# Moving part of a layer transition from VectorE to GpSimd, with new activation tables, gate slots and last PSUM banks

## The reference

```
xn = layernorm(x)
s = attention(xn)              # softmax over theta(qk), theta from sigmoid, tanh and relu
g = silu(xn + moe(layernorm(xn)))   # 8 experts, top 1, and a shared one
x = x + s * g                  # residual of layer 0
xn = layernorm(x)              # per row: mean, variance
s = mamba(xn)                  # conv, silu, softplus(delta), dA = exp(delta*A), scan over 512 steps,
                               # 16 states, 256 channels; y = sum_n C_n * h_n, + D*xv, @ W_out
g = silu(down(silu(gate(xn)) * up(xn)))   # int weights / 127
x = x + s * g
```

## Time and profile before

| | us |
|---|---|
| median of 3 runs | 743.29 |
| lowest, highest | 740.79, 745.15 |
| the profiled execution | 744.14 |
| its span | 742.3 |
| TensorE busy | 662.6 |
| VectorE busy | 630.6 |
| ScalarE busy | 514.7 |
| GpSimd busy | 476.0 |

### The profile page before, as it was taken

The page is one execution under the profiler, slowest core; times in us unless marked ns, Lnnn a source line. Parts: engine busy times, 40 slices in busy tenths (PEclk is TensorE's granted clock), DMA queues, the critical chain, the costliest instruction groups (busy, mean ns, idle before and its releaser), DMA issues.

```text
span 742.3 us, 12844 instructions
## 1 busy us (share of the span) xinstructions
PE 662.6 (89%) x3973; PEld 497.4 (67%) x3973; DVE 630.6 (85%) x1042; ACT 514.7 (69%) x1080; POOL 476.0 (64%) x292
## 2 busy tenths in 40 slices
PE   1898999999799998769999999999999999986885
PEld 0884556556555553346887887877868878876775
DVE  5768877777666663999999999999999999999996
ACT  1465666666544444789898799898998987987452
POOL 1000564000044554155898999999999999999997
PEclk9999999999999999989999999999999999999998
DMA  7900110001112215544634736365376356363300
GB/s 210 293 1 0 43 40 32 0 0 28 60 47 72 66 58 76 102 176 144 142 86 155 160 85 197 105 161 145 82 210 148 86 172 157 89 206 92 72 1 28
DMA packets 43432, 74.75 MB, mean 101 GB/s; under 512 B 6264, under 2 KB 30208, under 8 KB 41968
## 3 DMA queue, kind: packets, MB, share of 16 engines
q1 hardware_dynamic: 31744, 48.35, 20.3%
q0 software_dynamic: 9904, 25.12, 16.8%
q10 hardware_dynamic: 1728, 0.57, 0.3%
HBM read 46.01 MB, written 9.67 MB: 75 GB/s over the span
## 4 chain that ended last, share of the span: by engine, by line
PE 33%; POOL 29%; DVE 12%; issue 12%; DMA 9%; ACT 4%; SPq 1%; POOLq 0%; ACTq 0%; DVEq 0%
POOL nfT_all L1254 22%; DMA delta_e<-delta_e 7%; PE psum L1304 5%; PE psum L699 4%; PE psum L592 3%; PE psum L622 3%; PE psum L723 3%; POOL accP L1187 2%; POOL du L1239 2%; DVE xnT_all L1812 2%; PE psum L613 2%; PE psum L600 2%; PE psum L602 2%; PE psum L632 1%; PE psum L711 1%
## 5 line engine op out<-in xcount | busy, mean ns | idle before, releaser
L1812 DVE TENSOR_TENSOR_SCAN xnT_all<-psum,nfT_all 128x1024 f32<-128x1024 f32 x128 | 288.2, 2276 | 7.5 <-issue 5.3
L1304 PEld LDWEIGHTS psum<-W_out,xnT_all 128*128 128x128 f32 x2048 | 241.9, 194 | 45.5 <-issue 34.7
L1304 PE MATMUL psum<-W_out,xnT_all 128*128 128x128 f32 x2048 | 247.0, 278 | 14.7 <-DVE acc L1828 10.9
L1504 ACT ACTIVATE psum<-delta_e,A 128x511 f32<-128x511 f32 x256 | 167.0, 693 | 32.0 <-DVE xnT_all L1812 32.0
L1254 POOL TENSOR_TENSOR nfT_all<-nf_rows,du 128x1024 f32<-128x1024 f32 x63 | 148.4, 2478 | 22.2 <-DVE nfT_all L1894 21.6
L1254 POOL TENSOR_TENSOR nfT_all<-attn_all,du 128x1024 f32<-128x1024 f32 x64 | 161.7, 2687 | 0.0
L573 POOL DMA_INDIRECT moe_dram<-xnT_all x39 | 37.7, 967 | 120.0 <-ACT xnT_all L829 120.0
L562 POOL DMA_INDIRECT xs_dram<-nf_rows,pos x32 | 33.1, 1033 | 78.3 <-DVE pos L883 59.2
L1828 DVE SCALAR_TENSOR_TENSOR acc<-psum,in_rows,acc 128x128 f32<-128x128 f32 x224 | 61.8, 337 | 0.9
L1304 PE MATMUL psum<-vo_all,W_taps 128*128 128x512 f32 (+3 forms) x128 | 59.2, 593 | 0.7 <-ACT vo_all L1536 0.7
L1304 PE MATMUL psum<-vo_all,wgu 128*128 128x512 f32 x96 | 47.6, 618 | 6.6 <-DVE hff L1907 5.6
(11 more groups left out here) (227 smaller groups left out, 1163.8 us busy)
## 6 DMA issues: line engine op xcount, KB each, us to landing
nf_rows<-bt_dram SPq DMA_DIRECT2D x32, 512.0 KB, 5.0
attn_all<-bt_dram SPq DMA_DIRECT2D x32, 512.0 KB, 4.1
delta_e<-rl_ab POOLq DMA_DIRECT2D x7, 1024.0 KB, 8.1
res_all<-early POOLq DMA_DIRECT2D x7, 1024.0 KB, 7.2
delta_e<-delta_e POOLq DMA_DIRECT2D x7, 512.0 KB, 7.4
xs_dram<-attn_all SPq DMA_DIRECT2D x4, 645.0 KB, 8.0
xnT_all<-xs_dram SPq DMA_DIRECT2D x39, 64.5 KB, 1.9
x_all<-in_x_dram SPq DMA_DIRECT2D x8, 256.0 KB, 6.7
```

What stands on the lines that cost most here:

```text
L1304: return nc.tensor.matmul(o, l, r, start=start, stop=stop)
L1504: ins = nc.scalar.activation(dA[:, i % RA, k, 1:L], delta[:, p, h, 1:L], ACT.Exp, scale=A[:, h, 2 * q + k:2 * q + k + 1])
L1812: nc.vector.tensor_tensor_scan(hring[:, i % R, :, :].rearrange("p n l -> p (n l)"), dA[:, i % RA, :, :].rearrange("p n l -> p (n l)"), dbx ...
```

## The change

GpSimd takes the gate products of batches 3 to 7 and the adds of batches 5 to 7. `g_w` gets four slots in the place of two. In the first preparation the touch of Exp is replaced by an explicit load of the table set `natural_log_exp_and_others`; `roots(2)` moves ahead of `skip_out` and `C_out` and is followed by a second such load; `turned(2)` moves behind the first `decay`. `gates(6)` moves ahead of `conv_silu(0, 1)`. VectorE's `clear()` moves to the start of its list, and `shifts(2)` moves from ahead of `drives` to behind `conv_gate(1)` of round 0. In the last round states 12 and 13 go to banks 4 and 5, which are free once `gate()` has run, in the place of 6 and 7.

```
-            g_w = over[:, 4 * L:6 * L].rearrange("p (r l) -> p r l", l=L)
+            GW = 4
+            g_w = over[:, 0:GW * L].rearrange("p (r l) -> p r l", l=L)
+            def state_bank(b, n):
+                return bank[bM[n % 2]] if b == NB - 1 and n >= NS - 4 else bank[Gb[n % 2]]
 # GpSimd
+                def gated(i):
+                    pool.wait_ge(F["si"], i + 1)
+                    pool.wait_ge(F["sg"], i)
+                    pool.wait_ge(F["x1"], i - 1)
+                    nc.gpsimd.tensor_tensor(sg[:, i % 2, :], g_w[:, i % GW, :],
+                                            attn_all[:, i * TPB:(i + 1) * TPB, :].rearrange("p j d -> p (j d)"),
+                                            ALU.mult).then_inc(F["sg"], 1)
+                def added(i):
+                    pool.wait_ge(F["sg"], i + 1)
+                    pool.wait_ge(F["x1"], i)
+                    x_rows = x_all[:, i * TPB:(i + 1) * TPB, :].rearrange("p j d -> p (j d)")
+                    nc.gpsimd.tensor_tensor(x_rows, x_rows, sg[:, i % 2, :], ALU.add).then_inc(F["x1"], 1)
                 for b in range(NB):
                     ...
+                    if b == NB - 2:
+                        gated(3)
+                gated(4)
+                for i in range(5, NB):
+                    gated(i)
+                    added(i)
 # TensorE, project(n)
-                        drained(pe, b, n - 2)
+                        if b == NB - 1 and n >= NS - 4:
+                            pe.wait_ge(S["G1"], at(b, "G1", 1))
+                        else:
+                            drained(pe, b, n - 2)
 # ScalarE, gates(i)
-                    if i >= 2:
-                        act.wait_ge(F["sg"], i - 1)
+                    if i >= GW:
+                        act.wait_ge(F["sg"], i - GW + 1)
 # ScalarE, first_preparation
                         ssm_out()
-                        nc.scalar.activation(touch[:, :], eps[:, :], ACT.Exp)
+                        nc.scalar.preload_act_table_set("natural_log_exp_and_others")
                         ...
+                        roots(2)
+                        nc.scalar.preload_act_table_set("natural_log_exp_and_others")
                         skip_out()
                         C_out()
-                        roots(2)
-                        turned(2)
                         act.wait_ge(F["col"], 1)
                         decay(b + 1, 1 - p, 0, True)
+                        turned(2)
                         decay(b + 1, 1 - p, 1)
 # ScalarE, start
                 gates(5)
+                gates(6)
                 conv_silu(0, 1)
-                gates(6)
                 gates(7)
 # VectorE, first_preparation
                         conv_gate(0)
-                        residual(4)
+                        moments_of(3)
+                        added(4)
                         conv_gate(1)
-                        residual(5)
+                        moments_of(4)
                         norms(1)
-                        residual(6)
+                        moments_of(5)
+                        moments_of(6)
                         ...
-                        residual(7)
+                        moments_of(7)
                         moments(2)
                         ...
-                        shifts(2)
 # VectorE, round_, behind conv_gate(1)
+                    if not end:
+                        shifts(2)
 # VectorE, start
+                clear()
                 residual(0)
                 moments(0)
                 norms(0)
-                clear()
                 residual(1)
                 residual(2)
                 moments(1)
-                residual(3)
+                added(3)
```

More of the change, by code:

```diff
@@ L1329, in project @@
                         pe.wait_ge(S["scan"], at(b, "scan", 2 * q + 2))
-                        drained(pe, b, n - 2)
+                        if b == NB - 1 and n >= NS - 4:
+                            pe.wait_ge(S["G1"], at(b, "G1", 1))
+                        else:
+                            drained(pe, b, n - 2)
                         for j in range(TPB):
                             for h in range(KH):
-                                ins = mm(bank[Gb[n % 2]][:, j * P:(j + 1) * P],
+                                ins = mm(state_bank(b, n)[:, j * P:(j + 1) * P],
                                          hring[:, (2 * q + h) % R, n % 2, j * P:(j + 1) * P], W_out[:, h, :],
@@ L1509, in gates @@
                     act.wait_ge(s_moe[i % 2], 16 * (i // 2 + 1))
-                    if i >= 2:
-                        act.wait_ge(F["sg"], i - 1)
-                    nc.scalar.activation(g_w[:, i % 2, :], res_all[:, i * TPB:(i + 1) * TPB, :]
+                    if i >= GW:
+                        act.wait_ge(F["sg"], i - GW + 1)
+                    nc.scalar.activation(g_w[:, i % GW, :], res_all[:, i * TPB:(i + 1) * TPB, :]
                                          .rearrange("p j d -> p (j d)"), ACT.Silu).then_inc(F["si"], 1)
@@ L1557, in scale_state @@
                     for j in range(TPB):
-                        ins = nc.scalar.activation(ts(i)[:, j, :], bank[Gb[n % 2]][:, j * P:(j + 1) * P], ACT.Copy,
+                        ins = nc.scalar.activation(ts(i)[:, j, :], state_bank(c, n)[:, j * P:(j + 1) * P], ACT.Copy,
                                                    scale=Cc[:, p, j, n:n + 1])
@@ L1745, in rows_of, with gated @@
                     return a[:, i * TPB:(i + 1) * TPB, :].rearrange("p j d -> p (j d)")
-                def residual(i):
+                def gated(i):
                     dve.wait_ge(F["si"], i + 1)
@@ L1750, in residual, with added @@
                         dve.wait_ge(F["x1"], i - 1)
-                    nc.vector.tensor_tensor(sg[:, i % 2, :], g_w[:, i % 2, :], rows_of(attn_all, i), ALU.mult)\
+                    nc.vector.tensor_tensor(sg[:, i % 2, :], g_w[:, i % GW, :], rows_of(attn_all, i), ALU.mult)\
                         .then_inc(F["sg"], 1)
+                def added(i):
                     dve.wait_ge(F["sg"], i + 1)
@@ L1755, in residual, with moments_of @@
                         .then_inc(F["x1"], 1)
+                def moments_of(i):
                     dve.wait_ge(F["x1"], i + 1)
@@ L1759, in residual @@
                     ins.then_inc(F["bn"], 1)
+                def residual(i):
+                    gated(i)
+                    added(i)
+                    moments_of(i)
                 linked = [0]
```

## The result

The changed kernel took 748.60 us (median of 6 runs, 746.99 to 749.98) against 744.75 us before (6 runs, 740.79 to 745.28): ratio 1.0065, 95% interval [1.0043, 1.0086]. The forecast was 742.8 us. The profiled execution has a span of 748.2 us in place of 742.3. Timed again later, the changed kernel came to 1.0039 [1.0018, 1.0060].

What follows compares the result with a forecast made beforehand. No engine was free in the rounds; the chain ScalarE's conv_silu(1, 1), conv_gate(1), TensorE, fifth scan set round 0. Gains of 0.39 us there and 0.15 at the end, called 0.5, took 743.29 to 742.8 us, range 740.7 to 744.7.

Steps and rivals of the forecast that it cites:

- T: Start of conv_gate(1) in round 0 on VectorE, 327.74 us before; forecast 327.35, 0.39 us earlier.
- VectorE's relief: First preparation: eight products and adds, 5.5 us, leave VectorE, nearly all hidden; moments(2) is done 2.3 us ahead of need.
- the 1.17 us of the gates: First preparation: four gate slots and moved gates let ssm_out start at 307.95 us, 1.17 us earlier.
- `shifts(2)` costs nothing: Behind conv_gate(1) in round 0: its 0.4 us on VectorE fits inside a slack of 0.78 us.
- The rival of the hold: First preparation: VectorE operations with two SBUF inputs stand still while GpSimd works; 743.8 us, chance 0.30.
- the slack of 0.78: Round 0: VectorE's 0.78 us wait for TensorE ahead of its fifth scan, taken as cover for shifts(2).
- Tables and order: ScalarE from ssm_out to T: one load and the touch go, root and reload precede C_out; still four loads.
- Table loads: First preparation: each explicit load costs 1.28 us as in the profile row, without the Trainium skill's drain of about 1.38.
- The end: Last round: states 12 and 13 start earlier, but GpSimd's sums bound the finish; gain 0.15 us, bounds 0 to 1.1.
- The rival of a slow clock at the end: Last 32 matmuls: new idle time on TensorE puts them at the slow clock; 743.6 us, chance 0.10.
- the loads on top: First preparation: the explicit loads add to existing ones or cost more than the row, about 2.8 us; 745.6, chance 0.05.

Runs made afterwards that it cites:

- w2_after_again: The changed kernel, unchanged, timed and profiled again: 746.69 us, ratio 1.0039 to the kernel before.
- x3: The changed kernel with all products and adds back on VectorE; slots, tables, order and banks stay changed: ratio 1.0025 to the kernel before.
- z4: The changed kernel with 16 warming matmuls in place of 13 and four more matmuls ahead of ssm: ratio 1.0042 to the kernel before.
- x1: The changed kernel with 16 warming matmuls in place of 13: ratio 1.0044 to the kernel before.
- y4: The changed kernel with ScalarE's old order and no tables named: ratio 1.0020 to the kernel before.
- w3: Kernel before plus four slots, moved gates(6), last banks, Exp/Ln set in old order, decays' table loaded early, 16 warming matmuls: 742.44 us, ratio 0.9984.
- x0: The kernel before, unchanged, timed and profiled again: ratio 0.9962 to itself.
- w1: The kernel before, unchanged, timed and profiled a third time: 744.31 us, ratio 1.0013 to itself.
- y1: The kernel before with four gate slots and only ScalarE's new order and tables in the first preparation: ratio 1.0014 to the kernel before.
- z3: The kernel before with four gate slots, the last banks and VectorE's early clear() only: ratio 0.9990 to the kernel before.
- x2: The changed kernel with shifts(2) back ahead of drives: ratio 1.0021 to the kernel before.

## Why the prediction was wrong

The forecast was 742.8 us, 0.5 less than before, in a range of 740.7 to 744.7; the changed kernel took 748.60, by the ratio 0.65% more than before. The mechanism of the forecast was a shift at T, and its size and sign were wrong. I go by w2_after_again and the first profile of before, whose convolutions are equal; the forecast for the fifth scan was 0.39 us earlier, it was 3.66 later. These 4.05 us are 2.87 ahead of one-plus, 0.08 from there to T, and 1.10 behind T.

**"VectorE's relief": the step that failed.** It took the residuals off VectorE at no price to the operations left there, and counted their lateness only against the need for `moments(2)`. I had one-plus starting at 314.3, 33.2 after the last scatter; in w2 it was 36.07, in x3 without GpSimd's work 34.36. `added(4)`, the place that I watched, was not held (0.69 us), but the operations ahead of it were: `moments(1)` took 4.1 to 4.6 us in place of 0.8, so `conv_gate(1)` came at 24.87 in place of the 23.9 that I had worked out. TensorE's gap grew from 3.08 to 3.96 us, and ssm ran in 2.56 and dt in 3.75 us in place of 1.91 and 1.95. `ssm_out` came at 28.19 in place of the 26.85 of my sum (28.02 before), so the 1.17 us of the gates were gone, and ScalarE then waited 0.93 and 0.44 us for dt. dt was slow in five of the seven profiles with GpSimd's products and adds and no added matmuls in the gap, and in none of the nine without; closing the gap (z4) restored ssm and dt, and brought one-plus to 34.63. So about half of the step is the clock and half the held operations by themselves. That is shown where the convolution was fast (x1, y4, w2: gaps of 3.9 to 4.3 us). ssm by itself is no sign: behind a fast convolution and a gap of 3.07 us it took 3.50 us in w3, without GpSimd's work, and 1.91 behind 3.08 in the kernel before; dt was at full clock in both. Where it was slow, as in the changed kernel's first profile, the gap is 2.2 us with and without GpSimd's work, ssm was slow in some of either kind, and why dt was slow in that profile stays open. In the sum this step is 2.9 us.

**"`shifts(2)` costs nothing": failed.** The rival of the hold had been thought of for the transition, and not for this operation, although GpSimd's drives run exactly there. It took 1.7 us in place of 0.18, the slack of 0.78 was used up, and T to the fifth scan grew by 1.10. The slack was itself a draw: it is 0.78 where `rows` took 4.07 us and 1.20 in x0 and w1, where it took 4.80 and 4.82.

**Tables and order: right as worked out, wrong as a bargain.** I had 13.05 us from one-plus to T; it is 13.13. `C_out` to first decay 1.42 (1.44 forecast), from there to T 7.0 (6.95). No load fell away behind one-plus; Tanh needed its own. But I paid these 2.3 us with 1.17 us at `ssm_out` and 1.4 at Ln, and only the second came. By its rows the order alone loses (y1, 1.5 us at the fifth scan): the root and its reload were put ahead of `C_out`, on which `deltas` hang.

**Table loads.** The two explicit loads took 1.28 us each. Behind the second, `skip_out` started 0.01 us after its end (321.69 + 1.28, then 322.98); behind the first ScalarE waited for TensorE here, and in z4 `abs_relu` started 0.01 us after it. So the row was right, and the drain that the Trainium skill puts on each switch ("ScalarE: Activation LUTs", section "What ACT_TABLE_LOAD costs") does not show.

**The end: right** (0.15 forecast, 0.2 measured). The rival of a slow clock at the end did not occur: the last 32 matmuls took 3.84 us in the changed kernel and in z3.

**The range.** All cases but one lay between 741.5 and 744.1 us; the loads on top, 745.6, had a chance of 0.05 and lay outside my own range. I treated the profile of before as typical, and the same kernel's later profiles have the fifth scan 2.6 to 2.8 us later. The baseline was low too: the first three runs gave 743.29, six gave 744.75, and that alone stands at the upper end of the range. The rival of the hold was the right mechanism, and by one of its own signs it came true (`moments(2)` ended at 318.5, past 317.0), but it was priced at 0.2 to 0.8 us: I held only `added(4)` and the normalizations, not `moments(1)` and the shift, and left out what lateness does to TensorE. How much of the 3 to 5 us each part makes in the median is not shown, since each kernel has one profile and the ratios of x2, x3 and y4 (1.0020 to 1.0025) lie within 0.4% of 1.

## What to carry to other kernels

Work moved to GpSimd costs VectorE time even where no data passes between them: look at every VectorE operation with two SBUF inputs, and every `tensor_scalar`, narrow ones too, that will run beside it, also beside GpSimd work that was there before and beside which something is now moved. An operation of 20 columns can cost as much as one of 512 then (1.71 us here, against 1.41). When a delay opens a gap in TensorE's work, price the matmuls behind the gap at the lower clock, and take a profile of the unchanged kernel twice before a difference of 1% is built on it.

## What the runs showed of the hardware

- The hold also meets operations with one SBUF tensor input: `tensor_scalar` of 128x128 (eight in 3.7 to 6.1 us beside GpSimd, 2.14 alone) and of 128x8 (2.37 us in w2, 0.17 alone). Row moments (0.86 to 0.87 us) and operations with a PSUM input (0.67 to 0.69 us) kept their durations beside GpSimd.
- Thirteen warming matmuls took 13.02 us in one profile and 11.32 in another of the same code. Where they took 13.02 (three profiles), the lower clock fell into them (0.51 from 281 to 284 us in the first profile of before) and the convolution took 7.11. Where they took 11.32 (eleven profiles), they ended 2.4 to 3.5 us before the first transpose, and the convolution behind ran at the lower clock for part of its time (8.7 to 10.2 us). With 16, it took 7.1 in all three kernels that had them.
- The same kernel, timed again beside itself, came out 0.38% faster, with a 95% interval that excludes no change.
